# Image cross attention of a six-layer kernel: weighing moved one slot later and ahead of the next scores, values computed in their own batch's slot

## The reference, cut to what matters

```python
def attention(q, k, v):
    scores = jnp.einsum('bqhd,bkhd->bhqk', q, k) * scale      # 16 heads of 16
    probs = jax.nn.softmax(scores, axis=-1)
    return jnp.einsum('bhqk,bkhd->bqhd', probs, v)
q = rms_norm(linear(x, q_w, q_b), norm_q_w)
k_img = rms_norm(linear(ctx_img, k_img_w, k_img_b), norm_k_img_w)   # 257 keys a batch
v_img = linear(ctx_img, v_img_w, v_img_b)
x = x + linear(attention(q, k_img, v_img) + txt_x, o_w, o_b)
```

## Time and profile before

| | |
|---|---|
| runs | 3391.09, 3385.73, 3385.80 us; median 3385.8 |
| the profiled execution | 3389.27 us, of it the span 3387.5 |
| mean granted TensorE clock | 0.994 of full speed |
| PE busy | 3319.5 us, 98% of the span |
| DVE busy | 2345.6 us, 69% |
| ACT busy | 1990.9 us, 59% |
| POOL busy | 1790.7 us, 53% |
| the image attention | from the start to about 917 us |

### The profile page before, as it was taken

The page is one execution under the profiler, slowest core; times in us unless marked ns, Lnnn a source line. Parts: engine busy times, 40 slices in busy tenths (PEclk is TensorE's granted clock), DMA queues, the critical chain, the costliest instruction groups (busy, mean ns, idle before and its releaser), DMA issues.

```text
span 3387.5 us, 103409 instructions
## 1 busy us (share of the span) xinstructions
PE 3319.5 (98%) x34657; PEld 2411.1 (71%) x34657; DVE 2345.6 (69%) x7548; ACT 1990.9 (59%) x6062; POOL 1790.7 (53%) x3697
## 2 busy tenths in 40 slices
PE   9999999999899999999999999999989899999999
PEld 7888888888666776777777777777756566666665
DVE  5678777877787657888887888778867744444443
ACT  5777777777566547777777777777765411111111
POOL 5666666666566437777777777777746400000000
PEclk9999999999999999999999999999999999999999
DMA  3111111111212241111111111111136610000000
GB/s 98 55 57 55 53 54 53 57 54 53 71 42 65 78 126 42 46 48 47 47 42 47 47 47 47 42 48 46 47 96 159 188 45 19 19 19 18 15 16 6
DMA packets 280328, 187.67 MB, mean 55 GB/s; under 512 B 117165, under 2 KB 277125, under 8 KB 280213
## 3 DMA queue, kind: packets, MB, share of 16 engines
q1 hardware_dynamic: 279925, 185.75, 19.2%
q10 hardware_dynamic: 288, 0.40, 0.1%
HBM read 145.61 MB, written 36.21 MB: 54 GB/s over the span
## 4 chain that ended last, share of the span: by engine, by line
PE 59%; DMA 2%; DVE 1%; issue 0%; SPq 0%; ACT 0%; POOL 0%; DVEq 0%; ACTq 0%; POOLq 0%
PE bank_e L2644 13%; PE c_ps_a L1012 7%; PE bank_e L2621 7%; PE b_ps_a L978 6%; PE s_ps_a L985 5%; PE out_ps_a L1038 3%; PE a_ps_a L989 3%; PE c_ps_a L989 2%; PE b_ps_a L989 2%; PE c_ps_a L1071 2%; PE out_ps_a L1022 2%; PE m_ps_r L2239 1%; PE c_ps_a L1050 1%; PE out_ps_a L1111 1%; PE c_ps_a L1061 1%; DMA by_dim_q_r<-scratch_q 1%
## 5 line engine op out<-in xcount | busy, mean ns | idle before, releaser
L1150 ACT ACTIVATE probs_a<-s_ps_a,neg_max_a 128x257 f32<-128x257 f32 x1024 | 472.6, 474 | 82.4 <-DVE neg_max_a L1275 77.7
L1204 POOL TENSOR_SCALAR probs_a<-probs_a,gated_a 128x256 f32<-128x256 f32 x1024 | 470.8, 479 | 26.5 <-POOL gated_a L1213 26.4
L1275 DVE TENSOR_REDUCE neg_max_a<-s_ps_a 128x1 f32<-128x257 f32 x1024 | 424.4, 414 | 0.0
L2670 ACT ACTIVATE gate_e<-bank_e 128x512 f32<-128x512 f32 x128 | 76.4, 597 | 493.1 <-PE bank_e L2644 493.0
L523 POOL TENSOR_SCALAR probs_i<-probs_i,inv_sum_i 128x256 f32<-128x256 f32 x512 | 243.2, 488 | 128.4 <-DVE inv_sum_i L687 123.8
L2602 POOL TENSOR_TENSOR inv_std_e<-var_eps_e,half_e 128x4 f32<-128x4 f32 x8 | 8.1, 1009 | 567.1 <-DVE var_eps_e L2684 567.1
L2787 DVE TENSOR_TENSOR hidden_e<-gate_e,bank_e 128x512 f32<-128x512 f32 x128 | 87.3, 688 | 292.2 <-PE bank_e L2644 290.7
L1274 DVE TENSOR_TENSOR self_s_a<-s_ps_a,mask_a 128x32 f32<-128x32 f32 x1024 | 185.9, 182 | 148.5 <-PE s_ps_a L985 148.5
L507 ACT ACTIVATE probs_i<-s_ps_i,neg_max_i 128x257 f32<-128x257 f32 x512 | 235.8, 474 | 69.1 <-DVE neg_max_i L758 67.4
L366 PE MATMUL a_ps_i<-w_k_i,ctx_t_i 128*128 128x256 f32 x1024 | 252.4, 389 | 5.2 <-issue 5.2
L1012 PE MATMUL c_ps_a<-w_v_a,ctx_t_a 128*32 128x256 f32 x4096 | 248.6, 383 | 0.0
(11 more groups left out here) (371 smaller groups left out, 8225.0 us busy)
## 6 DMA issues: line engine op xcount, KB each, us to landing
ctx_t_i<-in_ctx_t SPq DMA_DIRECT2D x128, 256.0 KB, 2.7
ctx_t_a<-in_ctx_t SPq DMA_DIRECT2D x128, 256.0 KB, 2.7
mask_a<-in_L_xattn_mask SPq DMA_DIRECT2D x512, 4.0 KB, 1.5
v_bd_a<-v_self_a SPq DMA_DIRECT2D x512, 8.0 KB, 1.8
x_tok_i<-in_x SPq DMA_DIRECT2D x32, 128.0 KB, 2.0
x_res_i<-in_x SPq DMA_DIRECT2D x32, 128.0 KB, 2.4
x_after<-y_tok_i SPq DMA_DIRECT2D x32, 128.0 KB, 1.7
x_tok_d<-x_after SPq DMA_DIRECT2D x32, 128.0 KB, 2.2
```

Of the source, the lines that this page charges most:

```text
L1150: act.activation(probs[:, t, :], s_ps[:, g, 0:K], ACT.Exp, bias=neg_max[:, t:t + 1], accum_out=row_sum[:, t:t + 1]).then_inc(exp_done, 1)
L1204: pool.tensor_scalar(probs[:, t, 0:2 * P], probs[:, t, 0:2 * P], gated[:, t:t + 1], 1.0, ALU.mult, ALU.mult).then_inc(probs_ready, 1)
L1275: dve.tensor_reduce(neg_max[:, 4 * f + g:4 * f + g + 1], s_ps[:, g, 0:K], AX.X, ALU.max, negate=True).then_inc(max_ready, 1)
```

## The change

W moves one slot later: in slot n TensorE weighs batch n-1, between T2 and S. V moves to its own batch's slot (values of n in slot n, not of n+1). As the turned weights are now read a slot later, they get two sets of buffers. The items change slots: the turned tokens move to b = 0 and y to b = 1 (b = 2 and 3 stay). The layer norm's statistics (L690 to L695) and power move to b = 3, one slot ahead of the normalisation; the chunk's tokens are loaded in b = 2. DVE inverts the first two sums ahead of L698 and the last two behind it, and in b = 0 the rows of the 257th key (L743, L746) stand between. The selection (L765 to L770) stands ahead of the next maxima, not behind them. All of `scale` is in b = 2, `code` in b = 0 (parts 0 and 1) and b = 1 (parts 2 and 3, y between them). GpSimd's `p_last` stands behind all four weight tiles, and `res_bias` moves to the end of b = 1. The loop's body is the slots 2, 3, 0, 1, one more slot is unrolled at the end, and the eight unread matmuls are gone. ACT waits for `p_last` ahead of the exponentials. The core of the diff:

```diff
     def tensor(pe, before, ahead):
+        def weigh(at):
+            pe.wait_ge(v_ready, at.count(0))
+            for r in range(2):
+                pe.wait_ge(turn_read[r], at.count(0))
...
+            last.then_inc(out_done, 1)
...
-                ge(pe, v_ready, at.count(0))
+            if at.live():
+                if at.live(-1):
+                    pe.wait_ge(v_ready, at.count(-1))
                 for r in range(2):
                     for c in range(2):
-                        last = pe.matmul(c_ps[:, r * D:r * D + D], ctx_t[at.b(1)][:, c, r * P:r * P + P], w_v[:, c, :], start=c == 0, stop=c == 1)
+                        last = pe.matmul(c_ps[:, r * D:r * D + D], ctx_t[at.b()][:, c, r * P:r * P + P], w_v[:, c, :], start=c == 0, stop=c == 1)
...
-            if isinstance(at.i, int) and at.n() == B - 1:
-                for _ in range(8):
-                    pe.matmul(b_ps[:, 0:D], w_k[:, 0, 0:P], w_k[:, 1, :], start=True, stop=True)
...
                 last.then_inc(turned[1], 1)
+            if at.live(-1):
+                if has_item(at):
+                    ge(pe, *item_out(at))
+                elif at.live(-2):
+                    pe.wait_ge(out_read, at.count(-2))
+                weigh(At(at.i, at.o - 1))
             if at.live(1):
                 pe.wait_ge(k_ready, at.count(1))
...
     def gpsimd(pool):
...
                 for i in range(T):
-                    if i == T - 1:
-                        if b == 0:
-                            ge(pool, p_last_t_ready, at.chunks(-1))
-                        pool.tensor_tensor(p_last[:, T * b:T * b + T], probs[:, :, 2 * P], inv_sum[:, :], ALU.mult).then_inc(p_last_ready, 1)
                     if i % 2 == 0:
...
+                if b == 0:
+                    ge(pool, p_last_t_ready, at.chunks(-1))
+                pool.tensor_tensor(p_last[:, T * b:T * b + T], probs[:, :, 2 * P], inv_sum[:, :], ALU.mult).then_inc(p_last_ready, 1)
...
     def vector(dve, ahead):
...
         def slot(at):
+            weights(at, 0)
             if at.live(2):
                 dve.wait_ge(k_full, at.count(2))
...
+            if at.b() == 0 and at.live(-1):
+                last_rows(At(at.i, at.o - 1))
+            weights(at, 1)
...
+            if at.b() == 3 and at.live_chunk(2):
+                statistics(at)
...
-            if at.b() == 1:
-                square_mean(at)
+            if at.b() == 2:
+                scale(at)
+            square_mean(at)
+            if at.b() == 0:
                 code(at, 0)
...
+                code(at, 1)
...
+            if at.b() == 1:
+                code(at, 2)
                 if at.live_chunk(-1):
...
                     dve.tensor_tensor(y_tok[:, :], item_ps, res_bias[:, :], ALU.add).then_inc(y_ready, 1)
+                code(at, 3)
...
+            if at.live(-1):
+                select(At(at.i, at.o - 1))
             if at.live(1):
                 for i in range(T):
                     dve.wait_ge(scores_done, at.count(1, T, T - 1 - i))
```

More of the change, by code:

```diff
@@ L293, in item_out, with every_slot @@
         b = at.b()
-        if b == 0:
+        if b == 1:
             return y_ready, at.chunks(-1)
-        return (None, xn_t_ready, q_raw, q_t_ready)[b], at.chunks(1)
+        return (xn_t_ready, None, q_raw, q_t_ready)[b], at.chunks(1)
     def has_item(at):
-        return at.live_chunk(-1) if at.b() == 0 else at.live_chunk(1)
+        return at.live_chunk(-1) if at.b() == 1 else at.live_chunk(1)
+    def every_slot(eng, first, turns, slot):
+        for n in range(first, 2):
+            slot(At(n // 4, n % 4))
+        with eng.Fori(0, turns) as i:
+            for o in range(2, 6):
+                slot(At(i, o))
+        for n in range(4 * turns + 2, B + 2):
+            slot(At(n // 4, n % 4))
     def load_ctx(sp, at, d):
@@ L356, in tensor @@
     def tensor(pe, before, ahead):
+        def weigh(at):
+            pe.wait_ge(v_ready, at.count(0))
+            for r in range(2):
+                pe.wait_ge(turn_read[r], at.count(0))
+                for f in range(2):
+                    for g in range(4):
+                        last = pe.matmul(out_ps[32 * g:32 * g + 32, f * 64:f * 64 + 64], v[at.b() % 2][:, r, f * P + 32 * g:f * P + 32 * g + 32],
+                                         probs_t[at.b() % 2][r][:, g * P + f * 64:g * P + f * 64 + 64], start=r == 0 and f == 0, stop=r == 1, skip_group_check=True)
+            if at.b() == 3:
+                pe.wait_ge(v_last_ready, at.chunks(0))
+                pe.wait_ge(p_rows_ready, at.chunks(0))
+                for f in range(2):
+                    last = pe.matmul(item_ps[:, f * P:f * P + P], v_last[:, f * P:f * P + P], p_rows[:, :, :].rearrange("p b q -> p (b q)"),
+                                     start=False, stop=True, skip_group_check=True)
+            last.then_inc(out_done, 1)
         def slot(at):
@@ L511, in gpsimd, with deviation @@
     def gpsimd(pool):
+        def deviation(at):
+            pool.wait_ge(ln_dve, at.chunks(2))
+            pool.tensor_tensor(inv_std[:, :], var_eps[:, :], half[:, 0:1], ALU.pow).then_inc(ln_pool, 1)
         def slot(at):
@@ new lines, in select @@
+        def select(at):
+            b = at.b()
+            dve.wait_ge(out_done, at.count(0))
+            dve.tensor_scalar(own[:, :, :], out_heads[:, :, 0, :], pair[:, 0:1], None, ALU.mult).then_inc(own_step, 1)
+            dve.wait_ge(own_step, at.count(0))
+            dve.scalar_tensor_tensor(out=attn_t[:, :, b * L:b * L + L], in0=out_heads[:, :, 1, :], scalar=pair[:, 1:2], in1=own[:, :, :], op0=ALU.mult, op1=ALU.add).then_inc(attn_step if b == 3 else out_read, 1)
+            if b == 3:
+                dve.wait_ge(attn_step, at.chunks(0))
+                dve.tensor_tensor(attn_t[:, :, :], attn_t[:, :, :], item_ps.rearrange("p (f n) -> p f n", f=2), ALU.add).then_inc(out_read, 1)
@@ L776, in groups @@
             with dve.Fori(first, last) as i:
-                for o in range(1, 5):
+                for o in range(2, 6):
                     slot(At(i, o))
+        statistics(At(-2, 3))
         slot(At(-1, 0))
@@ L785, in vector @@
         first_done()
-        for n in range(FIRST + 3, 1):
+        for n in range(FIRST + 3, 2):
             slot(At(n // 4, n % 4))
@@ L791, in vector @@
         groups(23, TURNS, False, 2)
-        for n in range(4 * TURNS + 1, B + 1):
+        for n in range(4 * TURNS + 2, B + 2):
             slot(At(n // 4, n % 4))
```

182 lines of the change are left out of this document (69 added, 113 removed).

## The result

The kernel after takes **3409.56 us** (median of four runs, 3407.07 to 3412.62) against 3385.77 of the kernel before (3385.73 to 3391.09): **ratio 1.0065, 95% interval 1.0053 to 1.0076**, so it is slower, by 18 to 26 us. I had forecast 3390.8 with a range of 3376 to 3401; the result lies above that, and above the dearest rival's 3403.3. The profiled execution of after is 3410.69 us with a span of 3408.9, 21.4 us above the span of before.

What follows compares the result with a forecast made beforehand. TensorE's order of work was taken as the bound. Per chunk -0.58 + 0.20 + 0.36 + 0.10 + 0.05 = +0.13 us, +4.0 over 30.5 chunks, ends +1.0: +5.0 on 3385.8, so 3390.8 us, range 3376 to 3401.

Steps and rivals of the forecast that it cites:

- What goes, 0.58: TensorE's three stops a chunk, at the loop's turn, W in b = 1 and b = 3, all vanish: 0.58 us less.
- rival 2: Loop's turn stays bare between S of b = 1 and K of b = 2: 0.24 a chunk, 3398.1 us; chance 0.14.
- One more change of shape, +0.20: TensorE changes tile shape once more a chunk, as the last key's product now stands ahead of S: +0.20 us.
- T in b = 0, 0.36: T waits for GpSimd's weights, whose sums stand behind the last key's rows on DVE: 0.36 us a chunk.
- W in b = 1, 0.05: W waits for y_tok behind a code pass on DVE, mostly covered: 0.05 us a chunk, between 0 and 0.25.
- T in b = 3, 0.10: T waits for four weight tiles queued behind the query power on GpSimd: 0.10 us a chunk, between 0 and 0.22.
- Rival 3: Each GpSimd collision with DVE is paid: stops of 0.92 a chunk, 3403.3 us; chance 0.14.
- Ends: +1.0: Start, last slots and clock together cost 1.0 us outside the steady chunks.
- The head, +0.4: At the start later tokens delay the first S, but slot 0 has no W: +0.4 us net, -0.6 to +1.6.
- The tail, -0.6: In the last slots T comes earlier, its sums not behind a selection: -0.6 us, between -1.5 and 0.
- The clock, +1.2: More idle TensorE at both ends may cost clock: +1.2 us, between 0 and 3, an estimate.
- The unread matmuls save nothing: In the last slots these matmuls lie ahead of a wait of T for GpSimd, so removing them gains nothing.

Runs made afterwards that it cites:

- r3: Kernel after with r2's edit and the code passes dealt out anew, so that one stands behind `y_tok`: 3390.51 us, a chunk 27.482.
- y1: Kernel after with `y_tok` ahead of both code passes of b = 1: 3410.14 us.
- r1: Kernel after with the last key's rows of b = 0 behind the last two sums and the query spreading: 3399.82 us.
- r2: Kernel after, in b = 0 the normalisation ahead of the key bias, the query spreading and last key's rows behind the mean square: 3402.01 us.
- t3: Kernel after, in the last slots the scalers' steps behind the weight sums and next-layer passes behind GpSimd's last weights: 3406.47 us.
- m2: r3 plus d1, t3 and, at the start, first scales later, chunk 1's tokens loaded earlier, statistics behind the first spread queries: 3383.16 us, ratio 0.9987 to before.
- n1: Kernel before without its eight unread matmuls in the last slot: 3390.8 us against 3387.87 of before.
- d1: Kernel after with the eight unread matmuls put back ahead of T of the last batch: 3406.59 us.
- m4: m2 with DVE's last passes reordered by when each can start and who waits for it: 3383.65 us, ratio 0.9985 to before.
- m3: m2 with the selection of batch 126 moved ahead of the next layer's passes: 3386.79 us, ratio 0.9997 to before.

## Why the prediction was wrong

The forecast of +5.0 us had the right sign and was short by 18.8 us of the medians. In the spans it is 16.4: 5.2 in the chunks, 9.6 in the ends, 1.7 in later layers, each rounded. By its own steps, with means over thirty chunks where nothing else is said:

- **"What goes, 0.58": right in kind, 0.05 too high.** W to K is gone, the queries are spread and the rows made long before S and L378 of b = 3 and b = 0. But the three stops of before are 0.24, 0.08 and 0.21, together 0.53: b = 3 lasts 7.12 and would need 6.91, where I had 7.15 and 6.89. *The loop's turn*, rival 2, costs 0.01 behind S, not 0.24.
- **"One more change of shape, +0.20": right.** L378 to S takes 0.64 (512.12 to 512.76) where L448 to K took 0.52: 0.12, which together with K's 0.10 is 0.22. (I read T to T2 as 0.42 across two slots; it is 0.44, so T2 to S costs 0.09 more.) The chunk without stops is 27.48 (r3); my terms give 27.41, the means 27.78 - 0.53 + 0.22 = 27.47. The Trainium skill, TensorEngine Tiling (Array Packing), Tiling Modes, has it that a change of the mode drains TensorE; these prices agree with it.
- **"T in b = 0, 0.36": the chain was right, its price short.** Predicted: sums at S + 3.71, T at S + 5.21. Measured: 3.71 and 5.22 (505.29 to 510.51), though the parts differ: 0.20 from DVE to POOL and 0.05 from POOL to PE where I had 0.15 in one place, and 1.10 for the two tiles where I had 1.02, so that the sums agree to 0.01 is in part luck. The stop is 0.38 in 21 chunks and 0.46 or so in nine, 0.41 in the mean. What the sum lacked besides is that a T that was waited for goes slower itself: T to T2 takes 0.50 instead of 0.44. The slot is 0.47 above that of r3.
- **"W in b = 1, 0.05": too small.** It is 0.15 to 0.17 in the 23 chunks with code passes and nothing in the seven without, 0.13 in the mean. I took the slack of T for W's: y's sum needs the item, which ends at the same time wherever T is wanted, and stands behind a code pass of 0.84 that starts 0.42 late. The rows of before had the pass and its wait; I did not put them in line with the item's end. y1 shows the cause by removing it, and the seven chunks without code passes show the same.
- **"T in b = 3, 0.10": too large.** 0.01 (6.403 against 6.393 in r3).
- Rival 3, *each collision is paid*, gave 0.92 of stops a chunk; measured 0.60 (0.465, 0.127 and 0.010). But its mechanism is there: two tiles took 1.10 beside three DVE passes (L739, L686, L693) and 0.94 beside the key bias L729, which is what they take alone, and r1 and r2, which differ by these passes, differ by 0.16 in the slot. The Trainium skill, GPSIMD Engine Reference, Key points, names contention with VectorE's instructions in a 2-port perf mode or with two SBUF inputs. The rows agree: the four tiles take 1.95 in r2, without the passes, and L729, one of whose two inputs lies in PSUM, slowed none of the 91 tiles of after that ran beside it alone (0.48 each).

So a chunk costs +0.305 (-0.53 + 0.22 + 0.60 is 0.29; 0.01 is unplaced), not +0.13, and thirty chunks 5.2 us more than I said. The larger part lies elsewhere:

- **"Ends: +1.0": this step failed.** Measured +10.6. *The head, +0.4.* I had the tokens behind the wait for `v_last`'s store, and took that wait at its place in the trace of before, 21.46. But the change also moves the first group of `scale` into a filling slot, where DVE waits 2.33 us for a load, ahead of the mean square and the copy that the store sends. The store left at 21.52 instead of 18.13, and the whole chain (copy, store, its wait, tokens 2.1 us, statistics, spread queries) moved with it, first S to 28.94. TensorE stood idle for 5.18 us, its granted clock fell to 1.2 GHz meanwhile, and K took 3.39. I followed each queue by itself and costed `scale` at nothing. *The tail, -0.6.* I credited T with not standing behind a selection, and did not ask which of DVE's extra tasks in the last slots now stand ahead of the sums: the scalers (a wait of 1.91, 0.37 in t3), the passes for the next layer beside GpSimd's last weights (four tiles 2.88, in m2 without them 1.84), and with W a slot later the selection of 126 ahead of the last W. Measured +4.9 for the stretch. Waits there went from 5.9 to 10.8 us, or from 8.3 if the unread matmuls are left out of before (n1). *The clock, +1.2,* had no row behind it: from 930 to 950 us the granted clock of after is 0.74 where before has 0.91, and from 10 to 46 us 0.86 against 0.95, but no run shows what that costs by itself.
- **"The unread matmuls save nothing": half right.** They fill a wait (n1). In after their lack came with half clock over the last W and y; in d1, with them, half clock fell on an earlier row.

What stays open: how much of the tail belongs to the order itself (m4 is still 2 us above before there), how much the clock alone costs at either end, and whether the order of before, mended too, would beat m4. By the rows its chunk would be 27.25 without all three stops, below the 27.48 of m4. But only that of b = 3 (0.21) is DVE's, and without it alone 27.57 are left; the loop's turn (0.24) and the wait for ACT's copies (0.08) need edits of another kind. None was tried.

## What to carry to other kernels

When a change moves an engine's tasks within a slot that is also unrolled, walk the first and the last slots by themselves, queue by queue and then across queues: a task that costs nothing in the steady state can wait there for a load, and everything behind it in that queue moves along, stores and loads of other queues too. Order a helper engine's queue by when each step can start and who waits for it, not by what belongs together; an early place is as bad as a late one if the step has to wait there (m3). And where a gain in one slot shows up as a loss in the next (y1, r2), look at what stands between the moved step and the next slot's critical step, and deal the filler out over all slots (r3).

## What the runs showed of the hardware

- A stop at TensorE can cost more than its idle time: in b = 0 of after, T takes 0.50 us to T2 in all thirty chunks instead of 0.44. It isn't so everywhere: the Ts of the last slots, behind waits of 1.24 to 3.45 us, take 0.46 or 0.47.
- GpSimd slows beside DVE by very different amounts, and it depends on the pass. Tiles of 128x256 f32 in after: 0.48 us alone, beside the key bias L729, the maxima or the selection; 0.58 in the mean beside the spreading L686; 0.67 beside L739, L686 and L693; 1.20 in the mean (1.04 to 1.37) beside the code pass L642. In the last slot the first three weight tiles took 0.48 each, two of them beside the next layer's statistics, and the fourth 1.52 beside the product pass L679: it alone makes the 2.88.
- TensorE's granted clock fell to 1.2 GHz at both ends: at the start within 5.18 us of idle, at the end behind 3.45 us of it. In after, by stretch, in the view of windows (PE busy, clock, DMA share, GB/s):

```profile
10.00:46.00 36.00, 26.56 (x189) 0.86 0.32 94
...
930.00:950.00 20.00, 14.52 (x137) 0.74 0.19 63
```

The same stretches of before are at 0.95 and 0.91, with 32.61 and 18.98 us busy. Between 2.4 and 1.2 GHz K is 1.99 or 3.39 long, W 0.65 or 1.08, y 1.13 or 2.07. Nearly the same idle time is not always followed by the same clock: behind 1.81 us of idle at 918.43 the V of after ran at full clock (1.89), behind 1.80 us at 919.86 that of d1 at half (3.48).
